# Gated linear attention on one Trainium2 core: when late blocks are normalised, where late tiles are routed, and what the last tile leaves out

## The chip, the cores and the metric

The kernel runs on one core of one Trainium2 chip. The metric is the device time of one execution in microseconds (us). The kernel before took 3134.39 us (median of 3 runs, 3131.98 to 3135.0).

The core has five engines, each with its own in-order queue of instructions: PE (TensorE, matrix products into PSUM banks), DVE (VectorE), ACT (ScalarE), POOL (GpSimd) and SP (SyncE, which only issues transfers here). Queues meet through semaphores: an instruction that needs another engine's result waits for a count, and everything behind it on its own engine waits with it.

## The reference

The whole program is two layers, eight steps on 2048 tokens of width 128. The change touches one function, which is called twice: the gated linear attention with routed experts (`_L0_ffn_ref` in the reference), after the first and after the second attention. Cut to what matters here:

```
H, DK, DV, N_EXP, CHUNK = (8, 64, 64, 4, 64)
def chunk_gla(q, k, v, gk, C=CHUNK):          # S_t = diag(exp(gk_t)) S_{t-1} + k_t^T v_t ; o_t = q_t S_t
    g = jnp.cumsum(gc, axis=1); g_last = g[:, -1]
    qg = qc * jnp.exp(g);  kg = kc * jnp.exp(-g)
    A = tril(qg @ kg.T);   o_intra = A @ vc
    ...
    def step(S, inp):
        kv, dec, qg_c = inp
        o_inter = jnp.einsum('thd,hde->the', qg_c, S)
        return (S * dec[..., None] + kv, o_inter)
...
e = jax.nn.softmax(x @ We, axis=-1)
_, idx = lax.top_k(e, 1)                      # the first of equal maxima
mask = jax.nn.one_hot(idx, N_EXP, dtype=x.dtype).sum(-2)
rw = e * mask
o = gla(q1, k1, v, gk1) + sum over experts of gla(q2 * fac, k2 * fac, v, gk2 * mfac)
o = o * lax.rsqrt(jnp.mean(o * o, axis=-1, keepdims=True) + EPS) * norm_w
o = o * (g * jax.nn.sigmoid(g))               # g = x @ Wga @ Wgb
return o.reshape(B, L, H * DV) @ Wo
```

The state S after the last tokens is read by nothing.

## The kernel before

`gla_ffn` works on tiles of 128 tokens (NT = 16, numbered 0 to 15) and on blocks of 512 tokens (NB = 4, four tiles each). The layer norm, the low-rank products and the routing are made by block, everything else by tile. The order of each engine is written out by hand: `on_pool`, `on_pe`, `on_dve` and `on_act` each have an entry part, and then a loop over the tiles. Of the loop's body most belongs to tile t (scores, output, state update) and the rest prepares tile t+1 (values, keys, queries, their transposes) and tile t+2 (gates).

- **Banks.** PSUM banks 0 to 2 are a ring: a list of uses (`TILE_USES` per tile, and the extra ones) takes them in turn, and a use waits until the one three places earlier has been read (`Ring.before`). In the entry part the ring is seven banks wide (`ENTRY_USES`). The first uses of the small ring wait for the last entry use of their bank: `cum0` of tile 1 takes bank 0, and the last entry use of bank 0 is `gp` of tile 0 (the 22nd in the list), which is read by `weigh_gate(0)` on DVE.
- **The entry.** ACT computes 1/deviation of blocks 2 and 3 (`norm.deviation(2)`, `(3)`; L128, L130) behind `sigmoid(0)`, as its last work before the loop. DVE waits for it in `norm.apply(2)` (L123), and `highest_logit(1)` and `weigh_gate(0)` (L1098) stand behind that on DVE.
- **Tile 0** (`LATE_BLOCKS`) turns blocks 2 and 3 and makes their low-rank products and logits.
- **Tile 1** (`MASK_TURNS`) routes the 12 tiles 4 to 15 at once. `choose_experts(1, others)` on DVE (L1067 to L1086, 15 small instructions) stands before `normalise(1)` (L1179), which PE's `project(1)` (L975) waits for. Behind `project(1)` PE turns the masks of blocks 1, 2 and 3 (L813, 12 transposes); ACT copies them.
- **Tile 2** (`SAME_EXPERTS`) makes, behind its `project`, which tokens of a tile share an expert: 12 products on PE (L820) and six instructions on DVE (`mask_same`, L1092, L1093). `cumulate(t+1)` (L854) waits for the block of its tile (`same_masked`).
- **Each tile**, the last too, updates the state: `update` and `update_dense` on PE (L955, L963), `add_state` and `add_state_dense` on DVE (L1169, L1174); and POOL makes `v_experts` (L756) for it a tile ahead.
- **First of equal maxima.** `choose_experts` makes the mask (prob equals the maximum), then walks over the experts with a copy and three pairs of instructions that keep only the first.

Other lines used below: `scores` L911, `spread_experts` L920, `state_decay` L1149, `mask_scores` L1156, `square` on ACT L1330, `sum_squares` L969, `turn_k1` and `turn_q1` L880, the gate's sigmoid L1259 to L1263.

## Time and profile before

| | before |
|---|---|
| median of 3 runs | 3134.39 us (3131.98 to 3135.0) |
| the profiled execution | 3127.79 us |
| its span in the profile | 3126.6 us |
| mean granted clock of PE | 0.939 of full |
| PE, DVE, ACT, POOL busy | 90%, 80%, 65%, 27% |

The span runs from the first to the last instruction; 1.2 us of the profiled execution lie around it. The views used are the timeline (start in us, duration in us, engine, line, operation, tiles with partitions x elements, number of instructions merged, and in brackets how long the engine stood idle before and who ended that) and the windows (for each stretch: its length, the busy time of PE, PE's weight loads, DVE, ACT and POOL with instruction counts, then the granted clock of PE as a share of full speed, the DMA share and GB/s). Full speed is 2.4 GHz, and 0.50 is 1.2 GHz. The ends of matmuls are modelled. A tile is taken from the start of its first scores (L911) to that of the next. The two linear attentions lie at about 675 to 1098 us and 1770 to 2192 us of the span.

### The profile page before, as it was taken

Reading aid. Unit: us, or ns where it says so; the run is one execution under the profiler, and the core shown is the slowest. Engines: PE = TensorE matmul, PEld = TensorE weight load, DVE = VectorE, ACT = ScalarE, POOL = GpSimd, SP = SyncE. Lnnn points to the kernel's source line nnn. Section 1 sums busy time; section 2 is a strip of 40 time slices with the busy share of each in tenths; the row PEclk is TensorE's granted clock in tenths of the full one; section 3 lists DMA queues with packets and bytes.
Section 4 is the critical chain, followed back from the end, with each engine's and each line's share of the span. In section 5 each row is a group of like instructions: output and inputs, shape, how many; then the busy total and the mean of one; then the engine's idle time right before and its main releaser. Section 6 shows DMA issues by size and latency. Waiting matters only on the chain. (4 is left out here: it accounts for less than half of the span.)

```text
span 3126.6 us, 57936 instructions
## 1 busy us (share of the span) xinstructions
PE 2814.4 (90%) x23088; PEld 1295.3 (41%) x23088; DVE 2495.0 (80%) x3276; ACT 2041.2 (65%) x3866; POOL 843.3 (27%) x978
## 2 busy tenths in 40 slices
PE   5999999978999969999999899999787798678788
PEld 1222222236666622222222366666332354356655
DVE  8999999955666679999999556666899856799544
ACT  4999999955555439999999555554766423645121
POOL 0100000012333301000000123333487571299510
PEclk6999999988999969999999889999999898888989
DMA  2000000000000010000000000000000000000000
GB/s 99 5 16 18 20 20 17 6 7 1 1 2 1 2 61 5 16 18 20 20 17 6 12 1 1 2 1 1 26 0 1 10 1 1 0 1 1 1 1 14
DMA packets 30216, 35.34 MB, mean 11 GB/s; under 512 B 13623, under 2 KB 24058, under 8 KB 29690
## 3 DMA queue, kind: packets, MB, share of 16 engines
q1 hardware_dynamic: 29754, 31.57, 3.5%
q8 instruction: 182, 2.98, 0.4%
q14 instruction: 88, 0.72, 0.1%
q10 hardware_dynamic: 192, 0.07, 0.0%
HBM read 19.16 MB, written 7.34 MB: 8 GB/s over the span
## 5 line engine op out<-in xcount | busy, mean ns | idle before, releaser
L420 DVE TENSOR_REDUCE max_parts<-banks 128x2 f32<-128x1024 f32 x1024 | 1169.0, 1218 | 18.8 <-PE banks L308 18.4
L510 ACT ACTIVATE probs<-banks 128x512 f32<-128x512 f32 x2048 | 1082.6, 599 | 73.9 <-PE banks L315 56.7
L308 PE MATMUL banks<-k_parts,q_parts 48*128 48x512 bf16 x2048 | 621.5, 396 | 48.4 <-DMA k_parts<-k_scratch 24.1
L315 PE MATMUL banks<-q_parts,k_parts 51*128 51x512 bf16 x2048 | 655.1, 386 | 6.6
L333 PE MATMUL banks<-probs,v_heads 128*9 128x256 f32 x8192 | 637.4, 382 | 7.5 <-ACT pv_copy L521 0.3
L315 PEld LDWEIGHTS banks<-q_parts,k_parts 51*128 51x128 bf16 x2048 | 148.0, 94 | 482.5 <-ACT probs L510 417.3
L550 POOL CAST neg_max_parts<-neg_max 128x8 bf16<-128x8 f32 x64 | 12.9, 201 | 1151.7 <-DVE neg_max L425 1151.7
L333 PEld LDWEIGHTS banks<-probs,v_heads 128*9 128x9 f32 x8192 | 123.8, 88 | 379.0 <-issue 340.4
L1495 POOL TENSOR_TENSOR state_times_c<-state,c_row 128x1024 f32<-128x1024 f32 x63 | 148.1, 2357 | 88.6 <-ACT c_row L1810 54.0
L1688 DVE TENSOR_TENSOR_SCAN state<-banks,state_carry,state 128x512 f32<-128x512 f32 x128 | 157.3, 1271 | 6.4 <-ACT banks L1805 4.3
L308 PEld LDWEIGHTS banks<-k_parts,q_parts 48*128 48x128 bf16 x2048 | 126.4, 94 | 79.2 <-DVE max_parts L420 50.0
L2111 ACT ACTIVATE silu_a<-banks 128x512 f32<-128x512 f32 x80 | 47.8, 597 | 170.2 <-PE banks L1940 170.0
L1573 PE MATMUL banks<-state_times_c,ident 128*128 128x512 f32 x256 | 129.3, 629 | 29.7 <-POOL state_times_c L1495 29.2
L763 POOL TENSOR_TENSOR state_middle<-state_end,state_decay 128x1280 f32<-128x1280 f32 x32 | 74.6, 2330 | 249.0 <-DVE state_decay L1149 249.0
L2647 PE MATMUL banks<-state_queries,ident 128*128 128x256 f32 x256 | 77.4, 469 | 54.4 <-POOL state_queries L2625 54.4
L2013 DVE TENSOR_TENSOR hidden<-silu_a,banks 128x512 f32<-128x512 f32 x80 | 54.8, 687 | 88.9 <-PE banks L1942 87.7
L1805 ACT ACTIVATE banks<-dt,neg_A 128x512 f32<-128x512 f32 x128 | 86.1, 687 | 45.9 <-DVE state L1688 44.3
L2619 POOL TENSOR_TENSOR state_decayed<-state,decay 128x512 f32<-128x512 f32 x64 | 109.8, 1716 | 12.4 <-DVE state L2681 11.0
L1296 ACT ACTIVATE exp_cum<-banks 128x512 f32<-128x512 f32 x64 | 38.4, 600 | 94.9 <-PE banks L854 94.9
L768 POOL TENSOR_TENSOR scores_dense<-scores_dense,scores_expert 128x1024 f32<-128x1024 f32 x32 | 75.7, 2366 | 84.0 <-DVE scores_expert L1156 84.0
L1955 PEld LDWEIGHTS banks<-ffn_weights,hidden 128*128 128x128 f32 x640 | 84.1, 195 | 29.6 <-issue 19.9
L756 POOL TENSOR_SCALAR v_experts<-v_tile,expert_mask 128x512 f32<-128x512 f32 x128 | 86.4, 695 | 20.6 <-ACT v_tile L1280 20.6
(473 smaller groups left out, 5029.0 us busy)
## 6 DMA issues: line engine op xcount, KB each, us to landing
outT_half<-pv_copy SPq DMA_DIRECT2D x252, 16.0 KB
prob_sums<-pv_copy SPq DMA_DIRECT2D x252, 2.0 KB
q_scratch<-qk_parts SPq DMA_DIRECT2D x8, 384.0 KB, 3.9
k_scratch<-qk_parts SPq DMA_DIRECT2D x8, 384.0 KB, 2.5
k_parts<-k_scratch SPq DMA_DIRECT2D x32, 96.0 KB
q_parts<-q_scratch SPq DMA_DIRECT2D x28, 96.0 KB
k_parts<-k_scratch SPq DMA_DIRECT2D x32, 64.0 KB
q_parts<-neg_max_rows SPq DMA_DIRECT2D x128, 3.0 KB
```

What stands on the lines that cost most here:

```text
L308: nc.tensor.matmul(Mb[m % 2][:, blk(x)], Q[p % 2][half_of(x, ROWS), tile(t)], K[p % 2][half_of(x, ROWS), blk(b)], start=True, stop=True).t ...
L315: nc.tensor.matmul(bank("exp", n, x)[:, :], K[p % 2][half_of(x, ROWS + PARTS), tile(t)], Q[p % 2][half_of(x, ROWS + PARTS), blk(j)], start ...
L333: i = nc.tensor.matmul(PVb[group:group + VD, cols], V[:, t + k, 2 * (s // NB) + x, :], PT[:, (n + k) % RING, x, cols], start=(t == 0 and c ...
L420: nc.vector.tensor_reduce(mxp[s % 2][:, :, u // NB, u % NB], Mb[m % 2].rearrange("p (x k) -> p x k", x=2), AX.X, ALU.max).then_inc(*maxed. ...
L510: nc.scalar.activation(PT[:, n % RING, x, :], bank("exp", n, x)[:, :], ACT.Exp, scale=float(HD) ** -0.5).then_inc(*exped.inc())
L756: i = nc.gpsimd.tensor_scalar(vm[q][:, :, e, :], v_t[q][:, :, :], mask[:, t, e:e + 1], 1.0, ALU.mult, ALU.mult)
L1495: nc.gpsimd.tensor_tensor(G[m % 2][:, :, :], F[m % 3][:, :, :], Cs[m % 2][:, :].unsqueeze(1).broadcast_to([128, 2, 512]), ALU.mult).then_i ...
L1573: nc.tensor.matmul(Yb[c][:, :], g.ident[:, :], G[m % 2][:, c, :], start=(n == 0), stop=(n == NS - 1)).then_inc(*summed.inc())
L1688: nc.vector.tensor_tensor_scan(f, decay_bank(m, c)[:, :], f, carry[:, c, n:n + 1], ALU.mult, ALU.add).then_inc(*scanned.inc())
L1805: nc.scalar.activation(decay_bank(m, c)[:, :], dt[:, c, unit_blk(m)], ACT.Exp, scale=negA[:, c, m % NS:m % NS + 1]).then_inc(*decay_made.i ...
L1955: i = nc.tensor.matmul(Yb[:, tile(c)], hs[:, r % 3, tile(c)], w["w2"][:, u, :], start=(u in first and c == 0), stop=(u in last), skip_grou ...
L2619: nc.gpsimd.tensor_tensor(SD[:, :, :, :], S[1 - s % 2][:, :, :, 0:HD], d, ALU.mult).then_inc(*decayed.inc())
```

## The change

- `norm.deviation(2)` and `(3)` stand before `exp_half(0)` on ACT, where they stood behind `sigmoid(0)`. In `ENTRY_USES`, `gp` of tile 0 and `logit` of block 1 change places, so that bank 0 is last read by `highest_logit(1)`.
- `choose_experts(1, others)` stands behind `add_x(1)`, where it stood before `normalise(1)`.
- The masks of blocks 1, 2 and 3 are turned in tiles 2, 3 and 4, one block each, before `project`; the products of same experts and `mask_same` follow one block each, behind `project` and `add_x`. POOL's `mask_rows` and ACT's `copy_mask` move along.
- The first of equal maxima is kept by a product with the column (4, 3, 2, 1), a maximum and a comparison, three instructions for seven. POOL makes the column with four memsets.
- Tile 15 has no state update on PE and DVE and no `v_experts` on POOL.

```
-EARLY, ROUTED_FIRST, ROUTED = 4, 17, 38
+EARLY, ROUTED_FIRST, ROUTED = 4, 13, 30
-LATE_BLOCKS, MASK_TURNS, SAME_EXPERTS = 0, 1, 2
+LATE_BLOCKS, LATE_ROUTING = 0, 1
+LATE_MASKS = {2: 1, 3: 2, 4: 3}
-              ... ("half", 0), ("logit", 1), ("gp", 0),
+              ... ("half", 0), ("gp", 0), ("logit", 1),
...
-            uses += [(u, t + USES_AHEAD.get(u, 1)) for u in TILE_USES if t + USES_AHEAD.get(u, 1) < NT]
+            tile_uses = [(u, t + USES_AHEAD.get(u, 1)) for u in TILE_USES if t + USES_AHEAD.get(u, 1) < NT]
+            if t in LATE_MASKS:
+                tile_uses = tile_uses[:-1] + [("mask", LATE_MASKS[t]), tile_uses[-1], ("same", LATE_MASKS[t])]
+            uses += tile_uses
...
-            uses += [(u, b) for u, at in (("mask", MASK_TURNS), ("same", SAME_EXPERTS)) if at == t for b in range(1, NB)]
... on_pool
+            for e in range(NEXP):
+                i = nc.gpsimd.memset(falling[:, :, e:e + 1], float(NEXP - e))
+            i.then_inc(*falling_made.inc())
...
-                if t == SAME_EXPERTS:
-                    for b in range(1, NB):
-                        mask_rows(b)
+                if t - 1 in LATE_MASKS:
+                    mask_rows(LATE_MASKS[t - 1])
                 decay_state(t)
                 add_scores(t)
-                if t + 1 < NT:
+                if t + 2 < NT:
                     mask_values(t + 1)
... on_pe
-                update(t, 0)
-                update(t, 1)
                 if after:
+                    update(t, 0)
+                    update(t, 1)
                     keys(t + 1)
...
-                update_dense(t)
                 if after:
+                    update_dense(t)
                     turn_k1(t + 1)
                     turn_q1(t + 1)
+                if t in LATE_MASKS:
+                    turn_mask(ring, LATE_MASKS[t])
                 project(t)
+                if t in LATE_MASKS:
+                    same_expert(ring, LATE_MASKS[t])
...
-                for b in range(1, NB):
-                    if t == MASK_TURNS:
-                        turn_mask(ring, b)
-                    if t == SAME_EXPERTS:
-                        same_expert(ring, b)
... on_dve, choose_experts
-                nc.vector.tensor_copy(et[:, r], mask[:, r, 0]).then_inc(*routed.inc())
-                for e in range(1, NEXP):
-                    dve.wait_ge(routed, done + 7 + 2 * e)
-                    nc.vector.tensor_tensor(mask[:, r, e], mask[:, r, e], et[:, r], ALU.is_gt).then_inc(*routed.inc())
-                    dve.wait_ge(routed, done + 8 + 2 * e)
-                    nc.vector.tensor_tensor(et[:, r], et[:, r], mask[:, r, e], ALU.add).then_inc(*routed.inc())
+                dve.wait_ge(falling_made, 1)
+                nc.vector.tensor_tensor(mask[:, r, :], mask[:, r, :], falling[:, :, :].broadcast_to([128, r.stop - r.start, NEXP]), ALU.mult).then_inc(*routed.inc())
+                dve.wait_ge(routed, done + 9)
+                nc.vector.tensor_reduce(et[:, r], mask[:, r, :], AX.X, ALU.max).then_inc(*routed.inc())
+                dve.wait_ge(routed, done + 10)
+                nc.vector.tensor_tensor(mask[:, r, :], mask[:, r, :], up(et[:, r]), ALU.is_equal).then_inc(*routed.inc())
... on_dve, the loop (add_state and add_state_dense only if after)
-                if t == MASK_TURNS:
-                    choose_experts(1, others)
                 normalise(t)
                 add_x(t)
+                if t == LATE_ROUTING:
+                    choose_experts(1, others)
...
-                if t == SAME_EXPERTS:
-                    for b in range(1, NB):
-                        mask_same(ring, b)
+                if t in LATE_MASKS:
+                    mask_same(ring, LATE_MASKS[t])
... on_act
             softplus(1)
+            norm.deviation(2)
+            norm.deviation(3)
             act.wait_ge(zeroed, 1)
             exp_half(0)
...
             sigmoid(0)
-            norm.deviation(2)
-            norm.deviation(3)
...
-                if t == MASK_TURNS:
-                    for b in range(1, NB):
-                        copy_mask(ring, b)
+                if t in LATE_MASKS:
+                    copy_mask(ring, LATE_MASKS[t])
```

ACT, the end of the entry of the first linear attention, before. `ln_rstd` is 1/deviation of a block, `gate_sigmoid` belongs to tile 0:

```order
L1275 ACTIVATE abs_logit<-abs_logit 128x1024
L1302 ACTIVATE exp_halves_130<-banks 128x40
L1307 COPY k_decayedT_128<-banks 128x512
...
L1263 ACTIVATE gate_sigmoid<-gate_sigmoid 128x512
L128 ACTIVATE ln_rstd<-ln_mean_var,eps_ln 128x4
L130 ACTIVATE ln_rstd<-ln_rstd 128x4
L1296 ACTIVATE exp_cum<-banks 128x512
```

The same place in the changed kernel:

```order
L1279 ACTIVATE abs_logit<-abs_logit 128x1024
L128 ACTIVATE ln_rstd<-ln_mean_var,eps_ln 128x4
L130 ACTIVATE ln_rstd<-ln_rstd 128x4
L1306 ACTIVATE exp_halves_131<-banks 128x40
L1311 COPY k_decayedT_129<-banks 128x512
...
L1267 ACTIVATE gate_sigmoid<-gate_sigmoid 128x512
L1300 ACTIVATE exp_cum<-banks 128x512
```

The four small instructions (two pairs; one pair stands in the rows) moved past eight others, to before the copies of the first transposes.

DVE, the end of tile 1 and the start of tile 2, before. `expert_tmp` to `half_mask` is the routing of tiles 4 to 15, `outT_tile` is `normalise(1)`, `scores_dense` is `mask_scores(2, 0)`:

```order
L1174 TENSOR_TENSOR state_end<-state_middle,banks 128x4x64
L1067 TENSOR_REDUCE expert_tmp<-expert_prob 128x12
...
L1081 TENSOR_TENSOR expert_mask<-expert_mask,expert_tmp 128x12
L1083 TENSOR_TENSOR expert_tmp<-expert_tmp,expert_mask 128x12
L1086 TENSOR_SCALAR half_mask<-expert_mask,half_col 128x12x4 x2
L1179 TENSOR_TENSOR outT_tile<-outT_tile,out_square 128x512
L1183 TENSOR_TENSOR x_tok<-x_tok,banks 128x128
L1149 TENSOR_TENSOR state_decay<-exp_halves_131,exp_halves_130 128x20
L1156 TENSOR_TENSOR scores_dense<-banks,tri 128x512 x2
```

And in the changed kernel:

```order
L1178 TENSOR_TENSOR state_end<-state_middle,banks 128x4x64
L1183 TENSOR_TENSOR outT_tile<-outT_tile,out_square 128x512
L1187 TENSOR_TENSOR x_tok<-x_tok,banks 128x128
L1071 TENSOR_REDUCE expert_tmp<-expert_prob 128x12
...
L1083 TENSOR_TENSOR expert_mask<-expert_mask,falling 128x48
L1085 TENSOR_REDUCE expert_tmp<-expert_mask 128x12
L1087 TENSOR_TENSOR expert_mask<-expert_mask,expert_tmp 128x48
L1090 TENSOR_SCALAR half_mask<-expert_mask,half_col 128x12x4 x2
L1153 TENSOR_TENSOR state_decay<-exp_halves_132,exp_halves_131 128x20
L1160 TENSOR_TENSOR scores_dense<-banks,tri 128x512 x2
```

The routing moved from before `normalise(1)` to between `add_x(1)` and `state_decay(2)`, and has four instructions fewer.

PE, the end of tile 2, before. `outT_tile` is `project(2)`, the product of `expert_maskT` is that of same experts, then tile 3 begins with its scores:

```order
L880 MATMUL banks<-ident,q_decayed 128x128 x4
L975 MATMUL banks<-ffn_weights,outT_tile 128x128 x4
L820 MATMUL banks<-expert_maskT 128x128 x12
L911 MATMUL banks<-q_decayedT_127,k_decayedT_129 128x128 x8
L854 MATMUL banks<-log_decay_132,cum 128x512
```

And in the changed kernel:

```order
L885 MATMUL banks<-ident,q_decayed 128x128 x4
L818 MATMUL banks<-ident,expert_mask 4x128 x4
L980 MATMUL banks<-ffn_weights,outT_tile 128x128 x4
L825 MATMUL banks<-expert_maskT 128x128 x4
L916 MATMUL banks<-q_decayedT_128,k_decayedT_130 128x128 x8
L859 MATMUL banks<-log_decay_133,cum 128x512
```

Four transposes and four products stand here for the 12 products; the same two groups stand at the ends of tiles 3 and 4, and the 12 transposes at the end of tile 1 are gone.

## Rows read from the trace of the kernel before

**Rows 1.** The page: busy us, share of the span, instructions.

```profile
PE 2814.4 (90%) x23088; PEld 1295.3 (41%) x23088; DVE 2495.0 (80%) x3276; ACT 2041.2 (65%) x3866; POOL 843.3 (27%) x978
```

**Rows 2.** Windows, tiles 0 to 4: length, PE, PEld, DVE, ACT, POOL, clock.

```profile
713.87:749.36 35.49, 31.13 (x265) 20.14 (x265) 18.59 (x37) 19.43 (x37) 8.63 (x7) 0.90 0.00 1
749.36:778.30 28.94, 25.86 (x245) 17.39 (x244) 18.40 (x42) 14.33 (x27) 9.19 (x8) 0.94 0.01 1
778.30:804.07 25.77, 25.77 (x258) 18.09 (x257) 16.87 (x26) 14.02 (x26) 9.82 (x10) 1.00 0.01 2
804.07:828.61 24.54, 24.54 (x233) 15.82 (x232) 16.89 (x27) 13.41 (x24) 8.63 (x7) 0.93 0.01 1
828.61:851.50 22.89, 22.89 (x234) 15.34 (x233) 15.28 (x24) 13.30 (x24) 8.63 (x7) 1.00 0.01 1
```

**Rows 3.** Windows, tiles 1 to 3 of the second linear attention.

```profile
1844.49:1873.35 28.86, 25.78 (x246) 16.97 (x245) 18.40 (x42) 14.58 (x27) 9.36 (x9) 0.94 0.01 2
1873.35:1899.16 25.81, 25.81 (x258) 18.14 (x257) 16.88 (x26) 13.88 (x25) 9.69 (x9) 1.00 0.00 1
1899.16:1922.05 22.89, 22.89 (x231) 15.43 (x231) 16.90 (x27) 13.31 (x24) 8.64 (x7) 1.00 0.01 1
```

**Rows 4.** Timeline of PE, start of tile 0, first; last row second linear attention.

```profile
713.87 1.16 PE L911 MATMUL banks<-q_decayedT,k_decayedT 64*128 64x128 f32 x16 [0.77 <-ACT q_decayedT L1319]
719.15 2.08 PE L854 MATMUL banks<-log_decay,cum 128*128 128x512 f32 x2 [4.12 <-DVE out_gateT L1098]
724.10 0.39 PE L920 MATMUL banks<-expert_mask_rows,expert_select 4*128 4x128 bf16 x4
...
1813.79 2.08 PE L854 MATMUL banks<-log_decay,cum 128*128 128x512 f32 x2 [3.21 <-DVE out_gateT L1098]
```

**Rows 5.** Timeline of ACT and DVE, same place, first linear attention.

```profile
714.92 0.63 ACT L1263 ACTIVATE gate_sigmoid<-gate_sigmoid 128x512 f32<-128x512 f32 x1
...
716.01 2.14 DVE L123 TENSOR_SCALAR ln_normed<-x_tok,ln_mean_var,ln_rstd 128x128 f32<-128x128 f32 x8 [7.26 <-ACT ln_rstd L130]
...
718.36 0.74 DVE L1098 SCALAR_TENSOR_TENSOR out_gateT<-banks,ffn_weights,gate_sigmoid 128x512 f32<-128x512 f32 x1
```

**Rows 6.** Timeline, the end of tile 1, first linear attention.

```profile
770.42 0.19 DVE L1067 TENSOR_REDUCE expert_tmp<-expert_prob 128x12 f32<-128x48 f32 x1
...
773.51 0.68 DVE L1179 TENSOR_TENSOR outT_tile<-outT_tile,out_square 128x512 f32<-128x512 f32 x1
774.25 1.98 PE L975 MATMUL banks<-ffn_weights,outT_tile 128*128 128x128 f32 x8 [3.08 <-DVE outT_tile L1179]
776.02 2.35 PE L813 MATMUL banks<-ident,expert_mask 128*4 128x128 f32 x12
```

**Rows 7.** Timeline, the end of tile 2, first linear attention.

```profile
801.20 2.94 PE L820 MATMUL banks<-expert_maskT 4*128 4x128 f32 x24
802.39 0.69 DVE L1092 TENSOR_TENSOR same_expert_cum<-banks,cum 128x512 f32<-128x512 f32 x1 [0.80 <-PE banks L820]
```

**Rows 8.** Window, the start of tile 3, first linear attention; columns as rows 2.

```profile
804.00:809.00 5.00, 5.00 (x26) 2.41 (x26) 3.35 (x7) 1.25 (x3) 2.33 (x1) 0.66 0.01 3
```

**Rows 9.** Timeline, tile 15: expert scores that wait for the mask of dense ones.

```profile
1080.83 1.29 DVE L1156 TENSOR_TENSOR scores_dense<-banks,tri 128x512 f32<-128x512 f32 x2 [0.71 <-PE banks L911]
1081.67 1.66 PE L911 MATMUL banks<-q_decayedT,k_decayedT 64*128 64x128 f32 x16 [0.87 <-DVE scores_dense L1156]
```

**Rows 10.** Timeline, the end of tile 15, first linear attention.

```profile
1091.18 2.25 PE L955 MATMUL banks<-v_experts,k_decayed 128*64 128x256 f32 x16
1091.98 0.63 ACT L1330 ACTIVATE out_square<-outT_tile 128x512 f32<-128x512 f32 x1
1093.36 1.13 PE L969 MATMUL banks<-out_square,head_ones 128*128 128x512 f32 x2
```

**Rows 11.** Timeline of PE, the end of tile 2: four transposes, then the project.

```profile
799.50 0.63 PE L880 MATMUL banks<-ident,q_decayed 128*128 128x128 f32 x4
800.11 1.16 PE L975 MATMUL banks<-ffn_weights,outT_tile 128*128 128x128 f32 x8
```

More of the change, by code:

```diff
@@ L642 @@
 ST = 1 + NEXP
-EARLY, ROUTED_FIRST, ROUTED = 4, 17, 38
+EARLY, ROUTED_FIRST, ROUTED = 4, 13, 30
 TILE_USES = "cum0 cum1 klow v q2 half g0 g1 k1 q1 rs tk0 tq0 tk1 tq1 out".split()
 USES_AHEAD = dict(rs=0, out=0, g0=2, g1=2)
-LATE_BLOCKS, MASK_TURNS, SAME_EXPERTS = 0, 1, 2
+LATE_BLOCKS, LATE_ROUTING = 0, 1
+LATE_MASKS = {2: 1, 3: 2, 4: 3}
 ENTRY_USES = (("turned", 0), ("glow", 0), ("low", 0), ("g0", 0), ("g1", 0), ("mask", 0), ("v", 0), ("klow", 0), ("q2", 0), ("same", 0), ("turned", 1),
-              ("cum0", 0), ("cum1", 0), ("glow", 1), ("low", 1), ("k1", 0), ("q1", 0), ("g0", 1), ("g1", 1), ("half", 0), ("logit", 1), ("gp", 0),
+              ("cum0", 0), ("cum1", 0), ("glow", 1), ("low", 1), ("k1", 0), ("q1", 0), ("g0", 1), ("g1", 1), ("half", 0), ("gp", 0), ("logit", 1),
               ("tk1", 0), ("tq1", 0), ("tk0", 0), ("tq0", 0))
@@ L662, in gla_ffn @@
         rw, rws, et = sb("expert_weight", [128, NT]), sb("expert_weight_scaled", [128, NT]), sb("expert_tmp", [128, NT])
-        half = sb("half_mask", [128, NT, 2, NEXP])
+        half, falling = sb("half_mask", [128, NT, 2, NEXP]), sb("falling", [128, 1, NEXP])
         tri_s = sb("same_expert_tri", [128, NT, 128], BF16)
@@ L1220, in on_dve @@
                     weigh_gate(t + 1)
-                add_state(t, 0)
-                add_state(t, 1)
                 if after:
+                    add_state(t, 0)
+                    add_state(t, 1)
                     decay_keys(t + 1)
                     dense_queries(t + 1)
-                add_state_dense(t)
-                if t == MASK_TURNS:
-                    choose_experts(1, others)
+                if after:
+                    add_state_dense(t)
                 normalise(t)
                 add_x(t)
+                if t == LATE_ROUTING:
+                    choose_experts(1, others)
                 if t == LATE_BLOCKS:
@@ L1377, in on_act @@
                     sigmoid(t + 1)
-                if t == MASK_TURNS:
+                if t == LATE_ROUTING:
                     exp_logits(1, others)
```

5 lines of the change are left out of this document (2 added, 3 removed).

## The prediction

> **What bounds the kernel now.** The page first: PE is busy for 90% of the span and no other engine comes near [rows 1]. The chain that ended last lies in later stages, so it says nothing of this one; the windows do. An undisturbed tile takes 22.89 us and PE is busy for all of them, at full clock, with DVE busy for 15.28 (the last row of [rows 2]). So a tile costs what PE has to do, and the question is where PE waits or runs slower. Tiles 0 to 3 of the first linear attention take 35.49, 28.94, 25.77 and 24.54 us [rows 2]; tiles 1 to 3 of the second 28.86, 25.81 and 22.89 [rows 3]. The timeline then shows the causes. In tile 0 PE stands idle for 4.12 us (3.21 in the second attention) before `cumulate(1)`, released by the gate on DVE [rows 4]. In tile 1 it stands idle for 3.08 us before `project(1)`, released by `normalise(1)`, and runs the project in 1.98 us [rows 6]. Tile 2 has 2.94 us of same-expert products [rows 7], and tile 3 begins with five microseconds at a granted clock of 0.66 [rows 8].
>
> **The entry.** Before, the chain is: gate's sigmoid done at 715.55, the deviations, `norm.apply` from 716.01, and the gate only at 718.36 [rows 5]. Now the deviations come earlier on ACT and DVE does `norm.apply` while PE still turns keys and queries; `cumulate(1)` no longer waits for the gate but for `highest_logit(1)`, which by then is long done. The gap of 4.12 us closes. Next late is the mask of the dense scores: the gate can run from about 715.6, so this mask begins at about 716.5. Tile 15 shows what follows such a mask: the expert scores start 0.84 us after it (1081.67 minus 1080.83) and take 1.66 [rows 9], so `spread_experts` could stand at about 719.0, where it stands at 724.10 [rows 4]: 5.1 us. If PE runs `cumulate` at half clock, as in the row (2.08 us for one product), only the gap is won: 4.1 us, and 3.2 in the second attention. I take the middle, 4.6 and 4.2 with an upper end of 5.1 for both: 8.8 us, between 7.3 and 10.2.
>
> The moved deviations take about 0.9 us of ACT (two pairs; the first fits in the 0.46 between 715.55 and 716.01), beside PE's half sums and `gate_project`. If that cover were gone the entry would be 0.9 us longer each time. The routing of block 0 loses four small instructions, 0.8 us at 0.2 each, while PE is still in the gate logits: nothing, at most 0.8 each time. POOL's four memsets stand where it waits for the layer norm: nothing.
>
> **The routing moved.** Tile 1 becomes an undisturbed one: 28.94 and 28.86 minus 22.89 are 6.05 and 5.97, together 12.0 us. In it lie the gap, the slow project and the 12 transposes (776.02 to 778.30) [rows 2, 3, 6]. What comes back is a wait in tile 2: the routing now stands before `state_decay(2)` and `mask_scores(2, 0)`, and behind those wait POOL's `decay_state` (which has slack) and PE's `scores(2, 1)`. It has 11 of the 15 instructions that took 3.09 us (770.42 to 773.51) [rows 6], so 2.27 us. DVE was idle for 0.71 before this mask [rows 9], so the mask is 1.56 late. PE has 0.87 idle in tile 15 because it has no `cumulate` there; `cumulate(3)` is about 2.0 us at full clock (half of two times 2.08), which leaves 1.1 of cover and 0.5 of delay. The scores that follow the mask closely then take 1.66 instead of 1.16 [rows 4, 9], another 0.5. I take 1.1 per attention (none to 2.1): 2.2 us.
>
> **Masks and same experts, one block per tile.** Each batch is four transposes and four products. The products took 2.87 for twelve (801.20 to 804.07), so 0.96 [rows 2, 7]. The mask transposes are shown only in the slow stretch, 0.76 for four [rows 6]; four full transposes take up to 0.63 at full clock [rows 11]. I take 0.5, so 1.46 a batch and 4.4 for three. The Trainium skill (TensorE: Matmul & The Clock Gate, Back-to-back issue gap) gives a sustained 81 ns for a matmul of 128 columns, an estimate of 0.32 for four; the sum would gain 1.1 us by it, over six batches. I stay with the rows, since these are fp32.
>
> After tile 2 one wait is added: `cumulate(4)` needs `mask_same(1)`. DVE starts it 0.23 after a block's products (802.39 minus 801.20 minus 0.96) [rows 7] and needs two instructions, about 1.3 us; `scores(3, 0)` covers 1.1 of the 1.5, so 0.45 is left. In tiles 4 and 5 nothing waits for it so early. That makes 4.8 per attention, 9.7 in all. What goes is the surplus of tiles 2 and 3: 2.88, 1.65, 2.92 and 0.00, together 7.45 [rows 2, 3]. Net cost 2.2 us, between 1.1 (transposes at 0.45, no wait) and 4.7 (at 0.76, the wait twice as long).
>
> **The last tile.** `square` ends at 1092.61, so `sum_squares` can start at about 1092.7 instead of 1093.36, behind the updates [rows 10]: 0.65, less in the second attention. But the updates are what PE had to do there, and between its last pieces it now idles. If the clock falls, the project takes 1.98 instead of 1.16, 0.8 more [rows 6, 11]. I take nothing, from 1.3 won to 1.2 lost for both. POOL's `v_experts` and DVE's three additions are beside the path.
>
> **The sum.** 8.8 + 12.0 - 2.2 - 2.2 + 0 = 16.4 us. The profiled execution took 3127.79 (1.19 around its span of 3126.6), so 3111.4 in such an execution. The median of the runs lies 6.6 above it, at 3134.39; the same difference gives 3118.0.
>
> **Rivals.**
> - *The clock falls behind each of the six batches.* For it: the tile behind the twelve products began at 0.66 of full clock though PE was busy all the time, and cost 1.65 us more [rows 2, 8]. Against: in the second attention the same products left the clock at 1.00 [rows 3], and a batch is now a third as long. Six times 1.65 is 9.9: a gain of 6.5, 3127.9. The Trainium skill (TensorE: Matmul & The Clock Gate, Why this matters for your kernels) names idle gaps between bursts as what makes throughput drop. By that rule no batch costs clock, since PE doesn't idle there, and the forecast stands; rows 8 show a fall without a gap, so the trace doesn't bear it out fully.
> - *The entry's wait stays.* If something else that ends as late holds `cumulate(1)`, the 8.8 are missing: 7.6 gained, 3126.8. Against: no reader of its banks is later than the copies of the transposes, by the order of uses.
> - *More.* Both entries at their upper end (1.4), the last tiles at theirs (1.3), and block 0's shorter routing on the path (1.6): 20.7 gained, 3113.7.
> - *Slower.* The slow stretch behind a batch lasts, and PE, which has no slack in a tile, carries it whole. Tile 0 has 7.1 us at half clock (0.10 of 35.49, doubled) [rows 2], 3.5 lost. Six times 3.5 is 21: 4.6 slower than before, 3139.0. It decides from 2.7 lost per batch (16.4 by six). Against: the longest stretch behind such products cost 1.65.
>
> **How the numbers follow.** Forecast 0.71, with a range of its own of 12 to 20 us gained; clock at each batch 0.12 (often in part, which lies between); entry's wait 0.05; more 0.10; slower 0.02. The range of 8 in 10 goes from 3112 to 3125: it takes in the third rival and half of the first. A difference of 0.2% is 6.3 us, about what a measurement of this kernel can tell from no change. Faster by more: the forecast, the third rival, and most of the first two, 0.92; within: 0.06; slower: 0.02.
>
> **What would show it.** Right: no idle time of PE above 1 us between the first scores and `cumulate(1)`; tile 1 at 22.9 us; in tile 2 an idle time of about 0.5 us before `scores(2, 1)`, released by the dense mask; tiles 2, 3 and 4 at about 25.9, 24.4 and 24.4 us; clock at 1.00 in them. Wrong: a tile 2 above 27 us (the routing holds up more than one mask), windows below 0.95 behind the batches, or `cumulate(4)` waiting over 1 us for `same_expert_tri`.

## The result and the profile after

The changed kernel takes 3110.9 us (median of 4 runs, 3109.15 to 3112.69) beside 3133.18 for the kernel before in the same session (4 runs, 3126.18 to 3135.0). The ratio is 0.9932, 95% interval 0.9918 to 0.9945: clearly faster, as forecast, but by 22 us instead of 16. The time lies 1.1 us below the range.

The profiled execution took 3111.8 us. On its page, beside [rows 1], PE is busy for 9 us less and its share is the same 90%. The span is 16.0 us shorter; the rest of that was idle time of PE.

```profile
PE 2805.1 (90%) x23024; PEld 1292.6 (42%) x23024; DVE 2489.3 (80%) x3254; ACT 2043.0 (66%) x3866; POOL 839.6 (27%) x978
```

The windows of tiles 0 to 4 (length, busy time of PE, PEld, DVE, ACT and POOL, clock) answer to [rows 2]:

```profile
715.49:745.64 30.15, 29.64 (x265) 19.78 (x265) 16.29 (x27) 18.58 (x33) 8.65 (x7) 1.00 0.00 1
745.64:768.52 22.88, 22.88 (x233) 15.33 (x232) 15.35 (x25) 13.46 (x25) 8.65 (x7) 1.00 0.01 2
768.52:793.89 25.37, 24.87 (x246) 16.87 (x245) 17.53 (x36) 13.77 (x25) 9.25 (x8) 1.00 0.01 2
793.89:818.56 24.67, 24.38 (x245) 16.63 (x244) 16.48 (x26) 13.78 (x25) 9.25 (x8) 1.00 0.01 1
818.56:842.88 24.32, 24.32 (x246) 16.64 (x245) 16.48 (x26) 13.77 (x25) 9.25 (x8) 1.00 0.01 2
```

Tile 0 lost its gap, tile 1 became an undisturbed one, tiles 2 to 4 carry one batch of masks each, and the clock is 1.00 in all five. The second linear attention has the same five lengths within 0.01. Tiles 5 to 14 together take 228.14 us in both kernels.

At the entry, PE's timeline shows `cumulate(1)` (L859) right behind the first scores, at full clock. The first row of [rows 4] took 1.16 too, but `cumulate(1)` came 4.12 us later and took 2.08.

```profile
715.49 1.16 PE L916 MATMUL banks<-q_decayedT,k_decayedT 64*128 64x128 f32 x16 [0.77 <-ACT q_decayedT L1323]
716.58 1.12 PE L859 MATMUL banks<-log_decay,cum 128*128 128x512 f32 x2
717.54 1.02 PE L859 MATMUL banks<-log_decay,same_expert_cum 128*128 128x512 f32 x2
718.79 1.66 PE L916 MATMUL banks<-q_decayedT,k_decayedT 64*128 64x128 f32 x16 [0.23 <-DVE scores_dense L1160]
720.38 0.39 PE L925 MATMUL banks<-expert_mask_rows,expert_select 4*128 4x128 bf16 x4
```

DVE at the same place: the gate (L1102) is no longer behind `norm.apply`, and the mask of the dense scores follows it [rows 5].

```profile
717.20 0.75 DVE L1102 SCALAR_TENSOR_TENSOR out_gateT<-banks,ffn_weights,gate_sigmoid 128x512 f32<-128x512 f32 x1 [4.29 <-ACT gate_sigmoid L1267]
717.87 0.17 DVE L1153 TENSOR_TENSOR state_decay<-exp_halves,exp_halves 128x20 f32<-128x20 f32 x1
717.96 1.28 DVE L1160 TENSOR_TENSOR scores_dense<-banks,tri 128x512 f32<-128x512 f32 x2
```

The wait that the moved routing brings, in tile 2. DVE runs the routing from L1071 to L1090 and only then the mask; PE idles 0.39 us before `scores(2, 1)` (the third row), which then takes 1.75:

```profile
768.84 0.20 DVE L1071 TENSOR_REDUCE expert_tmp<-expert_prob 128x12 f32<-128x48 f32 x1
...
771.25 1.28 DVE L1160 TENSOR_TENSOR scores_dense<-banks,tri 128x512 f32<-128x512 f32 x2
...
771.99 1.75 PE L916 MATMUL banks<-q_decayedT,k_decayedT 64*128 64x128 f32 x16 [0.39 <-DVE scores_dense L1160]
```

One batch of masks, at the end of tile 2 (`turn_mask` L818, the project L980, `same_expert` L825), and the wait for it (the last row, `cumulate(4)`), to be read beside [rows 7]:

```profile
791.26 0.60 PE L818 MATMUL banks<-ident,expert_mask 128*4 128x128 f32 x4
...
792.80 1.15 PE L825 MATMUL banks<-expert_maskT 4*128 4x128 f32 x8
...
795.34 1.12 PE L859 MATMUL banks<-log_decay,cum 128*128 128x512 f32 x2 [0.29 <-DVE same_expert_tri L1097]
```

And the last tile, which answers to [rows 9] and [rows 10]. The updates are gone, `sum_squares` (L974) waits for `square` on ACT (1.44 us idle), and the products of scores and values (L954), those of the expert queries and the state (L941) and the project (L980) take 1.98, 3.61 and 2.07 us, where at full clock they take 1.09, 1.98 and 1.16 (rows of the filled last tile, below):

```profile
1078.33 1.98 PE L954 MATMUL banks<-scores_dense,v_tile 128*64 128x128 f32 x16 [2.69 <-POOL scores_dense L774]
1080.24 3.61 PE L941 MATMUL banks<-q_experts,state_middle 64*64 64x128 f32 x64
1085.29 1.12 PE L974 MATMUL banks<-out_square,head_ones 128*128 128x512 f32 x2 [1.44 <-ACT out_square L1334]
1088.58 2.07 PE L980 MATMUL banks<-ffn_weights,outT_tile 128*128 128x128 f32 x8 [2.17 <-DVE outT_tile L1183]
```

### The profile page after: what moved, and what is told of

It is laid out like the page before. It is cut to its first block and busy times, and to the rows that moved or that the text cites. A ratio compares the mean times of both kernels' runs of the same rounds, so it can differ in the third digit from the quotient of the medians.

```text
span 3110.6 us, 57788 instructions
## 1 busy us (share of the span) xinstructions
PE 2805.1 (90%) x23024; PEld 1292.6 (42%) x23024; DVE 2489.3 (80%) x3254; ACT 2043.0 (66%) x3866; POOL 839.6 (27%) x978
## 5 line engine op out<-in xcount | busy, mean ns | idle before, releaser
L1958 PE MATMUL banks<-ffn_weights,hidden 128*128 128x128 f32 x640 | 87.0, 281 | 5.0 <-DVE hidden L2020 3.7
```

What stands on the lines that cost most here:

```text
L1958: i = nc.tensor.matmul(Yb[:, tile(c)], hs[:, r % 3, tile(c)], w["w2"][:, u, :], start=(u in first and c == 0), stop=(u in last), skip_grou ...
```

## Where the time went, over several executions

To read the miss, both kernels have to be seen in more than one execution. The experiments below gave three profiles of each. The table shows where the 22.8 us between the mean spans lie (us; a tile runs from its first scores to those of the next, and the last tile to the start of its addition to `x_tok`). Rows with three numbers give each profile, the others the mean of three; the difference is always that of the means.

```
                               before (3 profiles)       changed (3 profiles)     difference
tile 0, both attentions        71.70                     60.92                    -10.78
tiles 1 to 4, both            203.33                    194.48                     -8.85
last tile, both                37.32                     37.86                     +0.54
state-space scan          243.3 245.0 247.5         243.2 243.1 242.0              -2.50
stage after the scan      455.2 455.1 455.0         453.4 453.3 453.3              -1.77
all other stages                                                                   +0.56
span                   3126.6 3135.4 3132.8      3110.6 3108.6 3107.2             -22.80
```

The windows of the scan, which the change doesn't touch, explain its row. Two executions of the kernel before, and one of the changed kernel:

```profile
2228.46:2471.73 243.27, 194.74 (x488) 72.49 (x486) 227.06 (x196) 169.60 (x314) 186.58 (x83) 0.96 0.00 0
```
```profile
2230.67:2478.15 247.48, 199.91 (x488) 74.23 (x486) 227.28 (x196) 169.63 (x314) 186.63 (x83) 0.94 0.00 0
```
```profile
2213.63:2456.80 243.17, 195.26 (x488) 72.87 (x486) 227.16 (x196) 169.93 (x314) 186.64 (x83) 0.96 0.00 0
```

The same 488 matmuls, with DVE busy for the same 227 us, take 4.2 us longer when the granted clock is 0.94 instead of 0.96. Beside the clock only PE's own busy time (5.2 us more) and that of its weight loads (1.7 more) differ; DVE, ACT and POOL agree within 0.3. The 4.2 lie between two executions of one program, so three profiles of each don't tell how much of the 2.5 in this row comes with the change.

## The experiments

All are compared with the changed kernel unless said otherwise. Times are medians of the timed executions.

**The changed kernel again, twice.**

> The changed kernel once more. The first measurement gave 22.3 us between the medians, the two profiled executions only 16.0 (spans 3126.6 and 3110.6). Theory 1: the change is worth what the tiles show, 19.6 us in tiles 0 to 4 of both linear attentions less 2.8 in the two last tiles, so 16 to 18 us, and the rest is scatter of the kernel before (3126 to 3135). Rival: the profiled execution of the kernel before was an unusually short one, and the change is worth 21 us or more. Theory 1 expects a ratio of 0.9943 to 0.9950, the rival 0.9935 or less.

> The changed kernel once more, as it is. Theory (its executions, 3105.8 to 3112.7 so far, have no group 8 us higher as the kernel before has): again all within 3105 to 3113, median 3108 to 3111, while those of the kernel before lie at 3124 to 3128 and at 3131 to 3137. Rival (it has such a group as well, and chance kept it out of nine executions): one or two of these lie at 3115 to 3121.

Measured: 3108.34 (5 runs, 3105.76 to 3109.83; 0.9921 of the kernel before, 0.9907 to 0.9935), and in another session 3108.97 (6 runs, 3104.88 to 3114.48; 0.9938, 0.9924 to 0.9951). All 15 executions lie at 3104.9 to 3114.5, mean 3109.5, and one (3114.48) stands apart at the top, near the rival's 3115. So "no upper group" is too strong; if the changed kernel has one, it is rare. Of the two theories of the first text the rival held (a ratio of 0.9935 or less, the first profile of the kernel before an unusually short one). The medians differ by 22.3, 27.0 and 19.7 us in the three sessions; the next experiment shows why this varies.

**The kernel before, two more profiles.**

> The kernel before, profiled again. Its 11 timed runs lie in two groups: 8 at 3131 to 3137 us with a mean granted clock of 0.936 to 0.940, 3 at 3125.6 to 3128.0 with 0.938 to 0.941, and the profile that the prediction used (3127.8) is one of the lower group. Theory 1 (the linear attentions themselves fall to half clock more often in the usual executions, at the waits and the same-expert products that the change removes): an execution of the upper group shows tiles 0 to 3 longer than the 35.5, 28.9, 25.8 and 24.5 us of the first profile, by 5 to 9 us over both linear attentions. Rival (the difference lies in other stages, whose phase against the clock differs): the tiles within 1 us of the first profile, and the 6 to 9 us in the stages after the second linear attention.

> As before_b, a third profiled execution of the kernel before: the same two theories, and with two more executions a chance that at least one belongs to the upper group (3134 to 3137 us).

Measured: 3136.66 (span 3135.4, clock 0.935) and 3134.0 (span 3132.8, clock 0.937), beside 3127.79 with 0.939 in the profile of [rows 1]. The 40 executions of the kernel before that these sessions gave lie in two groups: 17 between 3124.1 and 3128.7, nearly all with a mean clock of 0.938 to 0.942, and 23 between 3131.3 and 3137.4, nearly all with 0.935 to 0.937. Their mean is 3131.3. The profile on which the prediction rests fell in the lower group. Where the longer executions lose their time is not one place: beside the first profile, tiles 0 to 4 of both attentions are 1.6 and 0.3 us longer, the two last tiles 1.9 and 0.9, and the scan 1.8 and 4.2. So neither of the two theories fits both profiles.

**The entry undone.** The deviations of blocks 2 and 3 back behind the sigmoid, and the two bank uses in the old order:

```diff
-("half", 0), ("gp", 0), ("logit", 1),
+("half", 0), ("logit", 1), ("gp", 0),
...
-            norm.deviation(2)
-            norm.deviation(3)
             ...
+            norm.deviation(2)
+            norm.deviation(3)
```

> The changed kernel, with the deviations of blocks 2 and 3 back behind the sigmoid and the two uses of the entry ring back in their old order. Theory 1 (the entry's wait is worth what the tiles show): tile 0 goes from 30.15 to between 35.0 and 36.0 us in both linear attentions, all other tiles stay within 0.1, and the time rises by about 11 us over the changed kernel. Rival (part of the gain of tile 0 came from elsewhere, a clock that happened to be full): tile 0 at 33 to 34 us and a rise of 6 to 8 us.

Measured: 3119.4 (6 runs, 3116.12 to 3119.85), 11.1 above the 3108.34 of the same session; 0.9955 of the kernel before (0.9941 to 0.9969). Its tile 0 takes 35.66 and 35.93 us, against 30.14 and 31.14, and the gap is back:

```profile
719.52 2.08 PE L859 MATMUL banks<-log_decay,cum 128*128 128x512 f32 x2 [4.12 <-DVE out_gateT L1102]
721.38 1.92 PE L859 MATMUL banks<-log_decay,same_expert_cum 128*128 128x512 f32 x2
```

The 5.5 us of the first attention are the idle time (4.12) and the slow clock of both products (4.00 instead of 2.14), less the 0.23 of idle time before the expert scores and part of their 1.66. The entry is worth 10 to 11 us, more than the 8.8 forecast.

**Which half of the entry?** First only the order of the bank uses undone, then only the deviations.

> The changed kernel with one half of the entry undone: the two bank uses of the entry stand in their old order, so cumulate(1) waits for the gate again; the layer norm's deviations stay early. In the changed kernel the gate ends at 717.95 where cumulate(1) starts at 716.58. Theory (the two halves of the entry are separate steps, each with its own place): the gate is no later than now, so PE idles about 1.4 us before cumulate(1), which then runs in 1.12 (full clock) or, if the gap takes the clock along, in 2.08: tile 0 between 31.2 and 32.6 us, and the kernel 2 to 5 us over the changed one. Rival (the order of the banks is the whole gain): the gap is the old one, 4.1 us, and tile 0 takes 35.7.

> The changed kernel with the other half of the entry undone: the deviations of the last two blocks stand behind the gate's sigmoid again; the banks stay in the new order. Theory: cumulate(1) starts about 1.1 us after the scores at full clock, with no gap, but DVE's layer norm runs until about 2.5 us behind the sigmoid, as in the kernel before, and holds up the gate and the mask of dense scores by 1.5 us: the expert scores start that much later behind an idle time of about 1.8 us, tile 0 takes 31.6 to 32.6 us, the kernel 2 to 5 us over the changed one. Rival (only the deviations matter): 35.7. Rival (only the banks matter): 30.15, no difference.

Measured with the banks' order undone: 3111.27 (4 runs, 3104.77 to 3117.07), tile 0 at 32.43 and 30.78 us. With the deviations undone: 3118.29 (4 runs, 3116.49 to 3119.01), tile 0 at 35.07 and 35.58. The changed kernel of that session has 3108.97, with 30.14 and 31.04. On the first the theory was right in the first attention; in the second nothing was lost, and the 2.3 us between the medians are not clear of the scatter. On the second the theory was wrong (it had 31.6 to 32.6), and the rival that only the deviations matter (35.7) was nearly right. PE's timeline shows why. Banks' order undone, first and second attention:

```profile
716.36 1.74 PE L859 MATMUL banks<-log_decay,cum 128*128 128x512 f32 x2 [1.35 <-DVE out_gateT L1102]
717.89 1.91 PE L859 MATMUL banks<-log_decay,same_expert_cum 128*128 128x512 f32 x2
...
1801.32 1.13 PE L859 MATMUL banks<-log_decay,cum 128*128 128x512 f32 x2 [1.35 <-DVE out_gateT L1102]
1802.29 1.02 PE L859 MATMUL banks<-log_decay,same_expert_cum 128*128 128x512 f32 x2
```

Deviations undone, PE and DVE:

```profile
719.31 2.08 PE L859 MATMUL banks<-log_decay,cum 128*128 128x512 f32 x2 [3.46 <-DVE expert_prob L1065]
...
716.83 2.14 DVE L123 TENSOR_SCALAR ln_normed<-x_tok,ln_mean_var,ln_rstd 128x128 f32<-128x128 f32 x8 [7.25 <-ACT ln_rstd L130]
718.88 0.17 DVE L1063 TENSOR_REDUCE expert_tmp<-banks 128x4 f32<-128x16 f32 x1
719.08 0.17 DVE L1065 TENSOR_TENSOR expert_prob<-banks,expert_tmp 128x16 f32<-128x16 f32 x1
```

`cumulate(1)` now needs `highest_logit(1)` (L1063, L1065), and on DVE that stands behind `norm.apply` just as the gate did. Whichever of the two it waits for, the cause is `norm.apply` ahead of it: DVE stood idle for 7.25 us until ACT had made the deviations, and only then began its 2.14 us. With the deviations early the old order of the banks costs 1.35 us of waiting, and the clock sometimes stays up behind it (second attention) and sometimes doesn't (first).

**The routing undone:** `choose_experts(1, others)` stands before `normalise(1)` again, and all else as in the changed kernel.

```diff
-                normalise(t)
-                add_x(t)
                 if t == LATE_ROUTING:
                     choose_experts(1, others)
+                normalise(t)
+                add_x(t)
```

> The changed kernel, with the routing of tiles 4 to 15 back in front of normalise(1). Theory 1 (its whole chain is PE's wait): tile 1 grows from 22.88 to between 25.2 us (the chain of 2.3 us alone) and 26.6 (with the project at half clock), tile 2 shrinks from 25.37 to about 24.4, as the wait for the dense mask goes; net 1.5 to 3 us per linear attention, 3 to 6 us in the time above the changed kernel. Rival (in the kernel before most of tile 1's surplus was the 12 transposes, so moving the routing is worth little): tile 1 below 24 us, less than 2 us in the time.

Measured: 3118.74 (7 runs, 3110.52 to 3123.19), 0.9955 of the kernel before (0.9939 to 0.997). Tile 1 takes 26.13 us in both attentions (22.88 in the changed kernel), tile 2 24.98 and 24.84 (25.37). PE's timeline at the end of tile 1:

```profile
768.54 2.07 PE L980 MATMUL banks<-ffn_weights,outT_tile 128*128 128x128 f32 x8 [2.30 <-DVE outT_tile L1183]
```

So the place of the routing is worth 3.25 us less the 0.39 to 0.53 that come back in tile 2: 2.7 to 2.9 per attention, 5.6 in all. The rest of the 6 us that tile 1 loses came with the transposes, which left it too, and with the four instructions saved. The median is 8 to 10 us above the changed kernel's of other sessions, more than the tiles give and than the 3 to 6 expected; the profiled execution had a clock of 0.937 and 247.5 us in the scan, like the upper group of the kernel before. Its lowest execution (3110.52) is 5.6 above the lowest of the changed kernel's fifteen (3104.88), close to what the tiles give.

**All masks in tile 2.** `LATE_MASKS = {2: (1, 2, 3)}`: twelve transposes and the products of three blocks together, as before the change, but all at the end of tile 2, where the changed kernel has one block each in tiles 2, 3 and 4.

> The changed kernel, with the masks of blocks 1, 2 and 3 all turned before the project of tile 2 and all same-expert products behind it (12 transposes, 12 products at one place). Theory 1 (batches cost their own work wherever they stand, but a long run of products with 4 rows lowers the clock): tile 2 about 22.9 + 1.0 + 3 x 1.44 = 28.2 us, at most 0.5 more for the mask instructions on DVE, tiles 3 and 4 at 22.9, and tile 3 at 24.5 in those executions where the clock falls; the time 0 to 4 us above the changed kernel. Rival (placement costs nothing either way): the sum of tiles 2 to 4 stays at 74.4 us within 0.3.

Measured: 3112.13 (4 runs, 3110.87 to 3112.79), 0.994 (0.9924 to 0.9957). Tiles 2 to 4 take 28.07, 24.53 and 22.88 us, together 75.48, where the changed kernel has 74.36. The window of the five microseconds behind the products has the granted clock of [rows 8] again (0.66, the third number from the end):

```profile
795.36:800.36 5.00, 5.00 (x27) 2.76 (x28) 3.28 (x7) 1.33 (x3) 2.33 (x1) 0.66 0.01 3
```

and that of the changed kernel behind its batch of four:

```profile
818.56:823.56 5.00, 5.00 (x43) 3.14 (x42) 3.37 (x7) 2.07 (x4) 2.33 (x1) 1.00 0.00 0
```

The work of the batches is nearly the same. The changed kernel's tile 4 less its tile 1 gives 1.44 us for one (24.32 minus 22.88). Without its batch tile 2 would take 23.93 there, so three together cost 4.14 here, 1.38 each. Split, they cost 0.2 more and the wait of 0.29; what they save is the slow stretch, 1.65 us in tile 3 (24.53 minus 22.88). Splitting is worth 1.1 us per attention in the tiles, and what it gains is clock. The second attention agrees (tile 3 at 24.49). The timed executions can't show 2 us: 0.994 here, 0.9921 to 0.9938 for the changed kernel.

**The last tile.** First the state updates put back into it:

```diff
+                update(t, 0)
+                update(t, 1)
                 if after:
-                    update(t, 0)
-                    update(t, 1)
                     keys(t + 1)
...
+                update_dense(t)
                 if after:
-                    update_dense(t)
```

(and POOL's `mask_values` and DVE's three additions with them).

> The changed kernel, with the state update of tile 15 put back on PE, DVE and POOL. Theory 1 (the update kept PE's clock up, without it the project runs at half clock): the project of tile 15 falls from 2.07 to about 1.16 us, the stretch from the last scores to the last sum into x_tok from 19.7 to about 18.2 us in both linear attentions, and the time falls by about 3 us below the changed kernel. Rival (the slow last tile has to do with where the tile falls in time, not with the update): the stretch stays at 19.5 or more, the time within 1 us or higher by the 0.3 to 0.7 us that the update stands in the way of the sum of squares.

Measured: 3109.38 (6 runs, 3106.39 to 3115.09), 0.9928 (0.9913 to 0.9943): no difference in the time. The profiles differ, though. With the updates the last tile takes 18.21 and 16.59 us; without them it took 18.42 to 19.73 in five of six, and 16.43 once. In the first attention, with the updates:

```profile
1077.26 3.39 PE L941 MATMUL banks<-q_experts,state_middle 64*64 64x128 f32 x64
1080.57 2.16 PE L960 MATMUL banks<-v_experts,k_decayed 128*64 128x256 f32 x16
1082.66 1.12 PE L974 MATMUL banks<-out_square,head_ones 128*128 128x512 f32 x2
...
1085.95 1.16 PE L980 MATMUL banks<-ffn_weights,outT_tile 128*128 128x128 f32 x8 [1.55 <-DVE outT_tile L1183]
```

The project runs in 1.16 here, and in 2.07 without the updates: work that nobody needs stood in front of a piece that then ran at full clock. How long the project takes can be read from DVE's idle time before the addition to `x_tok`, which waits for it. With the updates that is 1.25 us in all eight attentions profiled (three executions of the kernel before, and this one). Without them, and without filling, it is 1.25 to 1.53 in seven of sixteen and 2.16 or 2.17 in nine. The timed executions show no gain from leaving the updates out.

**Products that nobody reads, in the last tile.** Instead of the updates, PE gets three short groups of matmuls into free banks, one where it waits for the masked scores, one before and one behind `sum_squares`; nothing reads what they write.

```diff
+                if not after:
+                    pe.wait_ge(scores_masked, 4 * t + 4)
+                    for x in range(2):
+                        nc.tensor.matmul(Abank[x][:, :], g.xnT[:, tile(t)], w["Wp"][:, 0:512], start=True, stop=True)
                 intra(t)
...
+                if not after:
+                    nc.tensor.matmul(Abank[0][:, :], ...)
                 sum_squares(t)
+                if not after:
+                    for x in range(2):
+                        nc.tensor.matmul(Abank[x][:, :], ...)
```

> The changed kernel, with five extra matmuls of 128x512 in tile 15 whose results nothing reads: two while PE waits for POOL's sum of the scores, one before the sum of squares and two behind it. Theory 1 (in the last tile PE's idle stretches lower the clock, and work in them keeps it): the products of the experts' queries with the state fall from 3.6 to about 2.0 us, the product behind the sum of scores from 1.98 to 1.09, the project from 2.07 to 1.16, so the stretch from the last scores to the last sum goes from 19.7 to about 16.3 us and the time falls by 5 to 7 us below the changed kernel. Rival (the clock falls anyway, or the extra matmuls delay what stands behind them): the stretch at 19 us or more, no gain.

> The kernel that fills the last tile's idle time of PE with products nobody reads, once more, in a chip session with the changed kernel. Theory (it keeps the clock in the last tile, 16.2 us instead of 18.4 to 19.7, twice, and 2 to 4 us of that are lost again where the scan begins at another phase of the clock): 1 to 3 us under the changed kernel, its lowest execution 3 under. Rival (the 1.5 us seen first was chance): no difference of medians, within 1 us.

Measured: 3106.86 (5 runs, 3102.72 to 3108.01) and 3107.09 (5 runs, 3102.89 to 3108.82), ratios 0.9913 (0.9898 to 0.9928) and 0.9926 (0.9914 to 0.9938). The last tile takes 16.22 us in all four places, and the window has a clock of 1.00, where the changed kernel has 19.66 and 0.73:

```profile
1070.34:1086.56 16.22, 13.73 (x153) 8.46 (x152) 5.84 (x9) 2.59 (x5) 5.96 (x3) 1.00 0.00 1
```
```profile
1071.03:1090.69 19.66, 12.41 (x143) 9.82 (x142) 5.84 (x8) 2.60 (x5) 5.95 (x3) 0.73 0.00 1
```

The three slow pieces at full clock, in the filled last tile:

```profile
1077.64 1.09 PE L954 MATMUL banks<-scores_dense,v_tile 128*64 128x128 f32 x16 [0.46 <-POOL scores_dense L774]
1078.67 1.98 PE L941 MATMUL banks<-q_experts,state_middle 64*64 64x128 f32 x64
...
1085.36 1.16 PE L980 MATMUL banks<-ffn_weights,outT_tile 128*128 128x128 f32 x8 [0.45 <-DVE outT_tile L1192]
```

That is 5.4 us less in the two attentions than the changed kernel's mean of 37.86, but the medians are only 1.5 and 1.9 us lower than its medians of the same sessions (mean of ten executions 3106.0, against 3109.5 of fifteen). The profiles show where the rest went: the scan takes 245.0 and 247.5 us, 3.5 more than the 242.8 that the changed kernel has on average. This is the fastest version of the study; its interval and the changed kernel's overlap in each session.

## Why the prediction was wrong in the time, and what of it was right

**The step that failed is the last one of the sum**: "The median of the runs lies 6.6 above it, at 3134.39; the same difference gives 3118.0." It took the distance between one profiled execution and the median for a constant of the program, and so, without giving a reason, put at nothing what the change does to the stages that it doesn't touch. The distance is no constant: the kernel before has two groups of executions 8 us apart, its profile was one of the lower group (3127.79) and its median one of the upper. The changed kernel's profile (3111.8) lies 0.9 above its median (3110.9).

Over all executions the mean fell from 3131.3 to 3109.5, by 21.8. The forecast 3118.0 is 8.5 above the second of these: 3.1 because it starts from 3134.39, a median of the upper group, and 5.4 because it takes off 16.4 and not 21.8. The profiles put these 5.4 (6.4 over three of each) mainly in the untouched stages, 3.7, and in the entry, 2.0; the terms below have them one by one.

From first profile to first profile the change gained 16.0 us where 16.4 were forecast, and that agreement is luck. The entries gave 11.2 in that pair (forecast 8.8), tiles 1 to 4 gave 8.4 (7.6), the last tiles took 3.0 back (nothing forecast), and the other stages took 0.6.

**The entry, forecast 8.8 (7.3 to 10.2), was 10.8** over the profiles and 11.1 in the timed undoing. The mechanism stood in all its steps: no idle time before `cumulate(1)`, the mask 2.5 us behind the first scores (forecast 2.6), the expert scores behind it. The size was off where the prediction hedged between full and half clock for `cumulate(1)` and took the middle; even its upper end, 10.2, was 0.6 too low. The gap goes together with the low clock: without it both products run in 1.12 and 1.02, with it in 2.08 and 1.92. In two of the three profiles the second attention enters tile 0 at a low clock all the same and takes about 1 us more (31.14 and 31.04); its first scores take 2.08 instead of 1.16:

```profile
1798.10 2.08 PE L916 MATMUL banks<-q_decayedT,k_decayedT 64*128 64x128 f32 x16 [0.77 <-ACT q_decayedT L1323]
```

The sentence that `cumulate(1)` waits "for `highest_logit(1)`, which by then is long done" is true only together with the early deviations; the prediction didn't say what each half is worth alone. The shorter routing of block 0, put at nothing, shows nothing: the first tile 0 starts at 713.9 to 715.5 us before and 714.0 to 715.5 after.

**The routing, forecast 12.0 less 2.2.** Tile 1 came out at 22.88 (22.9). In tile 2 the idle time was 0.39 (forecast 0.5), and the slow scores after it took 1.75 (1.66). What the undoing shows is that about half of tile 1's gain belongs to the transposes and the four instructions. For the time that makes no difference; for a reader who wants only the routing moved it does.

**The masks, forecast a net cost of 2.2.** A batch cost 1.44 (forecast 1.46), and the wait for `mask_same(1)` 0.29 (0.45). Tiles 2, 3 and 4 came to 25.37, 24.67 and 24.32, against about 25.9, 24.4 and 24.4. Tiles 1 to 4 together gained 8.85 against 12.0 - 2.2 - 2.2 = 7.6. (The lower end of the masks' cost, 1.1, should have been 1.0.) Most of the difference is the surplus of tile 3 before, counted as 1.65 and 0.00 from [rows 2, 3]: in the six profiled attentions of the kernel before it is 1.65 four times and 0.33 twice (the window of tile 3 in [rows 3] ends 0.3 us too early), 2.4 for the two on average.

**The last tile, forecast nothing, was nothing** by the timed undoing, and 0.5 lost for both attentions by the means of the profiles. The reason given (the time saved is paid back by a project at half clock) is what the rows show. The kernel before's second profile is the fair partner, since there too the products of scores and values are slow (1.98 in both). Beside it `sum_squares` starts 0.43 us earlier after the tile's first scores, the project takes 2.07 instead of 1.16, and the tile is 0.49 longer (19.66 against 19.17):

```profile
1088.39 1.98 PE L949 MATMUL banks<-scores_dense,v_tile 128*64 128x128 f32 x16 [2.68 <-POOL scores_dense L768]
...
1095.78 1.13 PE L969 MATMUL banks<-out_square,head_ones 128*128 128x512 f32 x2
...
1099.07 1.16 PE L975 MATMUL banks<-ffn_weights,outT_tile 128*128 128x128 f32 x8 [1.55 <-DVE outT_tile L1179]
```

The products of scores and values and of the expert queries, slow in some executions of either kernel, the prediction doesn't mention. Its bound of 1.2 lost has no working.

**The other stages, forecast nothing, gave 3.7.** The scan and the stage after it, with 4.3 of it, hold no changed instruction. In the stage after the scan it is one group of 16 matmuls behind an idle time of 5.3 us. It took 6.78, 6.74 and 6.75 us in the kernel before and 5.10, 5.10 and 5.14 in the changed one:

```profile
2918.57 6.78 PE L2647 MATMUL banks<-state_queries,ident 128*128 128x256 f32 x16 [5.28 <-POOL state_queries L2625]
```
```profile
2903.53 5.10 PE L2650 MATMUL banks<-state_queries,ident 128*128 128x256 f32 x16 [5.27 <-POOL state_queries L2628]
```

It isn't bound to the kernel before: with the routing undone the group takes 6.77, and with the updates put back 6.70, at a clock of 0.55 instead of 0.72. In the six other variants profiled it takes 5.10 to 5.16. Its windows in the changed kernel and with the updates put back:

```profile
2901.57:2906.70 5.13, 5.10 (x16) 3.96 (x16) 0.00 (x0) 0.00 (x0) 0.00 (x0) 0.72 0.00 0
```
```profile
2897.69:2904.40 6.71, 6.70 (x16) 5.07 (x16) 0.00 (x0) 0.00 (x0) 0.00 (x0) 0.55 0.00 0
```

So the 6.4 us between 16.4 and 22.8 are: the entry 2.0, tiles 1 to 4 1.2, the last tile -0.5, and 3.7 in stages that the change doesn't touch.

**The rivals.** Clock falling behind each batch: refuted, the windows have 1.00 behind the batches of four. It does fall behind twelve products together (0.66 in the kernel with all masks in tile 2), so the two kernels stand on either side of whatever decides it. Entry's wait stays: refuted, though with the late deviations the wait stays at 3.46 us in spite of the new order of the banks. The slower case: nothing of it was seen. "More" (3113.7) named the right direction and, for the entry, the right reason.

**What stays open.** Why the kernel before is in the upper group in 23 of 40 executions and the changed kernel in none or one of 15. The scan's and the next stage's clock differ between executions of one program and between programs that differ only far ahead of them, so when the stage is reached seems to matter. No run shifted a stage by a chosen time, so that was argued and not tested.

## What to carry to other kernels

Before adding the distance between a profiled execution and the median to a forecast, look at the single runs: if they form two groups, forecast each group by itself and say which one the profile was in. When a wait names a small instruction of an in-order engine, price what stands ahead of it there: moving the waiter to another small instruction behind the same long one gains next to nothing. And a gap of PE costs more than its length where the matmuls behind it run at half clock, so closing it should be priced with them at full clock; conversely, taking away unneeded work that fills a gap can gain nothing.

## What was not expected of the hardware

- The twelve same-expert products in a row (2.94 us with PE busy throughout) were followed by a granted clock of 0.66 over 5 us in the first attention of both kernels that have them, though not each time: in two of the six profiled attentions of the kernel before the next tile lost 0.33 us and not 1.65. Batches of four were followed by 1.00.
- An idle time of 1.35 us before `cumulate(1)` was followed by products of 1.74 and 1.91 us in one attention and of 1.13 and 1.02 in the other of the same execution.
- One and the same program took between 3124.1 and 3137.4 us over 40 executions, in step with its mean granted clock (0.942 to 0.935).
- Five matmuls that nobody reads made the last tile 2.2 to 3.5 us shorter than it was in five of the changed kernel's six (16.22 against 18.42 to 19.73).
